# Expert tiles of a mixture of experts: 32 full tiles and four units of two half tiles in place of 39 tiles

## The reference, cut to what matters

```python
h = _L0_tok_ref(x, ...)                      # moving averages, then 128 -> 256
h = h + _L0_attn_ref(_layernorm(h), ...)
h = h + _L0_ffn_ref(_layernorm(h), ...)      # the experts
h = h + _L1_attn_ref(_layernorm(h), ...)
h = h + _L1_ffn_ref(_layernorm(h), ...)

def _L0_ffn_ref(x, gate_w, gate_b, w1, b1, w2, b2):
    probs = jax.nn.softmax(x_flat @ gate_w.T + gate_b, axis=-1)
    topk_vals, topk_idx = jax.lax.top_k(probs, 2)
    h = jax.nn.relu(jnp.einsum('nd,edh->neh', x_flat, w1) + b1)     # 256 -> 1024
    y = jnp.einsum('neh,eho->neo', h, w2) + b2                      # 1024 -> 256
    out_flat = jnp.einsum('ne,neo->no', dense_gate, y)
```

## Time and profile before

| what | before |
| --- | --- |
| median of 3 runs | 763.72 us |
| span of the profiled execution | 773.7 us |
| mean granted TensorE clock in it | 0.964 |
| TensorE busy | 701.8 us, 91% |
| VectorE, ScalarE, GpSimd busy | 444.4, 350.6, 147.4 us |
| expert stage, first to last product | 247.0 to 543.8 us |
| its 39 tiles | 7.24 us each in the steady part |
| attention, layer 1 | 543.8 to about 735 us |

### The profile page before, as it was taken

One profiled execution on the slowest core, in us unless ns is written; L12 is line 12 of the kernel. 1 busy time (PEld: TensorE's weight loads), 2 busy tenths in 40 slices (PEclk: granted clock), 3 DMA queues, 4 the chain that ended last, 5 costly groups with the idle time before them and its releaser, 6 DMA issues.

```text
span 773.7 us, 16147 instructions
## 1 busy us (share of the span) xinstructions
PE 701.8 (91%) x5671; PEld 576.0 (74%) x5681; DVE 444.4 (57%) x1129; ACT 350.6 (45%) x599; POOL 147.4 (19%) x180
## 2 busy tenths in 40 slices
PE   5697999999889999999999999999889999999855
PEld 4476777777767998999999999998556666665533
DVE  3567587778763542244322232233479988977686
ACT  2242453355335221212211212131779898899735
POOL 2010112331322021000000100200465553411000
PEclk9799999999998999999999999999999999999975
DMA  6979264466374566555555555574555774555002
GB/s 166 201 138 271 41 91 89 76 89 89 76 171 159 183 195 239 196 184 197 161 187 198 188 187 198 173 184 115 93 88 73 110 107 67 81 63 69 1 14 96
DMA packets 70839, 102.54 MB, mean 133 GB/s; under 512 B 8416, under 2 KB 58600, under 8 KB 70640
## 3 DMA queue, kind: packets, MB, share of 16 engines
q1 hardware_dynamic: 67376, 93.15, 50.4%
q0 software_dynamic: 3136, 8.40, 4.3%
q10 hardware_dynamic: 256, 0.07, 0.0%
HBM read 63.75 MB, written 12.58 MB: 99 GB/s over the span
## 4 chain that ended last, share of the span: by engine, by line
PE 65%; DVE 12%; DMA 8%; issue 5%; ACT 4%; POOL 2%; SPq 2%; ACTq 0%; DVEq 0%; POOLq 0%
PE psum L2102 18%; PE psum L2153 17%; DMA arena<-arena 7%; PE psum L2060 3%; PE psum L1782 3%; PE psum L2045 3%; PE psum L2074 3%; DVE arena L1346 2%; DVE arena L1199 2%; PE psum L1806 2%; POOL w0T L703 2%; PE psum L2051 1%; SPq L568 1%; PE psum L1811 1%; PE psum L2130 1%
## 5 line engine op out<-in xcount | busy, mean ns | idle before, releaser
L2102 PEld LDWEIGHTS psum<-arena 128*128 128x128 f32 x1248 | 144.9, 192 | 3.3 <-issue 1.7
L2102 PE MATMUL psum<-arena 128*128 128x128 f32 x1248 | 146.1, 275 | 1.2 <-issue 1.1
L2153 PE MATMUL psum<-arena 128*128 x624 | 141.3, 380 | 0.8 <-DVE arena L1492 0.8
L875 ACT ACTIVATE arena<-psum,arena 128x128 f32<-128x128 f32 x156 | 44.5, 368 | 190.1 <-PE psum L2102 106.6
L2153 PEld LDWEIGHTS psum<-arena 128*128 128x128 f32 x624 | 115.6, 190 | 15.3 <-issue 1.2
L1474 DVE TENSOR_SCALAR arena<-psum,arena 128x128 f32<-128x128 f32 x156 | 44.0, 344 | 81.0 <-PE psum L2102 64.8
L2060 PE MATMUL psum<-arena 96*128 96x256 bf16 x512 | 74.8, 276 | 8.4 <-ACT arena L845 4.2
L1346 DVE TENSOR_TENSOR arena<-arena 128x1024 f32<-128x1024 f32 x64 | 77.9, 1284 | 1.3 <-ACT arena L845 1.3
L1199 DVE TENSOR_REDUCE arena<-psum 128x6 f32<-128x768 f32 x64 | 59.3, 954 | 28.9 <-PE psum L1811 27.5
L703 POOL DMA_INDIRECT w0T<-yg,pos x32 | 40.3, 1260 | 185.6 <-DMA yg<-arena 177.4
L2060 PEld LDWEIGHTS psum<-arena 96*128 96x128 bf16 x512 | 44.8, 98 | 40.5 <-issue 14.7
(11 more groups left out here) (309 smaller groups left out, 1201.4 us busy)
## 6 DMA issues: line engine op xcount, KB each, us to landing
arena<-in_L_ffn_w_dram SPq DMA_DIRECT2D x47, 1024.0 KB
arena<-arena SPq DMA_DIRECT2D x192, 128.0 KB, 4.6
arena<-xg SPq DMA_DIRECT2D x39, 128.0 KB
yg<-arena SPq DMA_DIRECT2D x39, 128.0 KB, 1.7
out_dram<-arena SPq DMA_DIRECT2D x8, 256.0 KB, 2.1
xg<-zeros SPq DMA_DIRECT2D x9, 128.0 KB, 2.6
arena<-in_x_dram SPq DMA_DIRECT2D x8, 128.0 KB, 3.2
arena<-in_L_ffn_b_dram SPq DMA_DIRECT2D x1, 1024.0 KB
```

The lines of the kernel that those rows point to most:

```text
L875: ins = act.activation(hidT[:, v, c, :], psum[:, 2 * v, c * P:(c + 1) * P], ACT.Relu, bias=b1c[:, v, c:c + 1])
L2102: mm = pe.matmul(psum[:, 2 * v + c // HALF, (c % HALF) * P:(c % HALF + 1) * P], w1b[:, i % W1_BUFS, d, c * P:(c + 1) * P], xtT[:, v, d, :] ...
L2153: mm = pe.matmul(y_bank, hidT[:, u, c, :], w2s[:, one(e), c, :].rearrange("p o n -> p (o n)"), start=(c == 0), stop=(c == HC - 1))
```

## The change

**Units.** An expert's remainder of at most 64 rows goes to a half tile, one of over 64 to a full one. Then 32 full tiles and 8 half tiles suffice for any routing, and where more than 32 full ones would be needed, the surplus takes two halves each. Two half tiles, of two experts, make a pair. The stage runs 36 units: 8 early full tiles, then four times three full tiles and a pair (units 11, 15, 19 and 23), then 12 full tiles.

**A pair's first layer** has the tokens stationary (64 of them for each half) and the weights moving: 8 products of 512 columns, alternating between the halves, whose results stand in PSUM rows 0 to 63 and 64 to 127. ScalarE and VectorE copy these to `hid_raw`, TensorE transposes them back (8 transposes, behind the second layer of the unit before), and then each half gets the bias and relu of its own expert, 8 operations of 64 columns on each engine. The second layer is 16 products of 256 columns, alternating; the second half's weights are copied by VectorE to `w2p` before. A pair loads two sets of first-layer weights, with a fourth buffer `w1p` until the last pair has begun, and two blocks of 64 rows.

**The plan** sorts the late tiles so that those that the first three batches need come among the first 13, and lists 40 entries. `late_valid` has 7 steps where it had 3, `late_grid` 16 where it had 3, `late_list` 6 where it had 5; `slot_levels` has 8 steps where it had 4, `slot_counts` 8 where it had 6, `half_counts` is new with 3, and `tile_slots` has 17 where it had 7, now in iteration 15. `rank_tokens` keeps a copy of the counts for four batches of the first stage.

**Gathers.** The gather of batch 0 waits for 24 units, those of batches 1 and 2 for 25, and that of batch 3, for all 36, stands right behind that of batch 2, ahead of the attention's iterations. Combining and statistics of batch 2 are among the tiles now (iterations 33 and 34), and the steps of batches 0 and 1 are moved to fit. In the first stage the step that negated the row maxima is gone; the sign is applied in a copy on ScalarE.

```diff
+def unit_table():
+
+    units = [("full", t) for t in range(EARLY_TILES)]
+    for j in range(PAIR_UNITS):
+        units += [("full", EARLY_TILES + LEAD * j + n) for n in range(LEAD)] + [("pair", j)]
+    return units + [("full", t) for t in range(EARLY_TILES + LEAD * PAIR_UNITS, FULL_TILES)]
...
+    last, loads, table = [-1] * (W1_BUFS + 1), [0] * (W1_BUFS + 1), []
+    for i in range(UNITS):
+        mine = []
+        for _ in entries(i):
+            free = [n for n in range(W1_BUFS + (i < SPARE_UNTIL)) if last[n] != i]
+            n = min(free, key=lambda n: (last[n], n))
+            mine.append((n, loads[n] + 1, last[n] + 1))
+            last[n], loads[n] = i, loads[n] + 1
+        table.append(mine)
+    return table
...
-            e = sp.value_load(tile_e[0:1, i:i + 1], min_val=0, max_val=EXPERTS - 1)
-            sp.dma_start(w1b[:, i % W1_BUFS], a["L0_ffn_w1"][one(e), :, :].rearrange("o (c p) n -> p (o c) n", p=P)
-                         ).then_inc(w1_ld[i % W1_BUFS], 16)
+            for entry, (n, _, ready) in zip(entries(i), W1_OF[i]):
+                wait(sp, S["l1_hi"], ready)
+                e = sp.value_load(tile_e[0:1, entry:entry + 1], min_val=0, max_val=EXPERTS - 1)
+                sp.dma_start(w1_at(n), a["L0_ffn_w1"][one(e), :, :].rearrange("o (c p) n -> p (o c) n", p=P)
+                             ).then_inc(w1_ld[n], 16)
...
+            rows = P // len(entries(i))
+            for n, entry in enumerate(entries(i)):
+                r = sp.value_load(tile_row[0:1, entry:entry + 1], min_val=0, max_val=EXPERTS * CAP - P)
+                sp.dma_start(xt_in[n * rows:(n + 1) * rows, i % 2], xg[bass.ds(r, rows), :]).then_inc(x_ld[i % 2], 16)
...
-                    done = min(EARLY_TILES + 2 * EXPERTS, MOE_TILES) if b == 0 else min(2 * EXPERTS * (b + 1), MOE_TILES)
+                    late = FIRST_OF_0 if b == 0 else FIRST_TILES if b < FIRST_BATCHES else LATE_TILES
+                    done = LATE_ROW + late
...
-                for b in range(2):
+
+                for b in range(3):
                     gather(b)
                     scale1(b, 0, S["n_mv"], S["n_eps"], S["n_rstd"])
-                gather(2)
+                gather(3)
...
+                    pair = pair_of(i + 1)
+                    if pair is not None:
+                        act.wait_ge(S["l1_lo"], i + 2)
+                        wait(act, S["hid_mm"], pair)
+                        act.copy(hid_raw[:, 0:HID // 2], psum[:, 2 * v, :]).then_inc(S["hid_ev"], 1)
...
+                    if pair is not None:
+                        act.wait_ge(S["bias_done"], i + 2)
+                        act.wait_ge(S["hid_mm"], pair + 1)
+                        act.wait_ge(S["l2_mm"], i)
+                        for c in range(HALF):
+                            for n, bias in enumerate((b1c[:, v], b1p)):
+                                ins = act.activation(hidT[:, v, c, n * HALF_P:(n + 1) * HALF_P],
+                                                     psum[:, 2 * v, c * P + n * HALF_P:c * P + (n + 1) * HALF_P], ACT.Relu,
+                                                     bias=bias[:, c:c + 1])
+                        ins.then_inc(S["reluA"], 1)
...
+                    plan(dve.tensor_reduce(plan_s[:, 0:3], plan_place.rearrange("p (k e) -> p k e", e=EXPERTS), AX, ALU.add))
+                    plan(dve.tensor_reduce(plan_s[:, 3:6], plan_total.rearrange("p (k e) -> p k e", e=EXPERTS), AX, ALU.add))
+                    plan(dve.tensor_copy(plan_of[:], plan_total.rearrange("p (k e) -> p k e", e=EXPERTS)))
+                    plan(dve.tensor_tensor(plan_of[:, 0:2], plan_of[:, 0:2], over(chosen_of[:], 1, [P, 2, EXPERTS]), ALU.add))
+                    plan(dve.tensor_scalar(place_t, before_t, total_n, before_n, ALU.add, ALU.subtract))
...
+                    if pair is not None:
+                        a_e, b_e = (expert_of(entry) for entry in entries(i + 1))
+                        wait(dve, S["reluA"], i)
+                        dve.tensor_copy(b1c[:, v, :], b1T[:, :, one(a_e)].rearrange("p c o -> p (c o)"))
+                        dve.tensor_copy(b1p, b1T[:, :, one(b_e)].rearrange("p c o -> p (c o)")).then_inc(S["bias_done"], 1)
+                        dve.wait_ge(S["bias_done"], i + 2)
+                        dve.wait_ge(S["l1_hi"], i + 2)
+                        dve.tensor_copy(hid_raw[:, HID // 2:], psum[:, 2 * v + 1, :]).then_inc(S["hid_ev"], 1)
+                        wait(dve, S["l2_mm"], i)
+                        dve.tensor_copy(w2p, w2s[:, one(b_e)].rearrange("p o c n -> p (o c) n"))
...
+                        rows = P // len(entries(i))
+                        for n, entry in enumerate(entries(i)):
+                            e = expert_of(entry)
+                            at = slice(n * rows, (n + 1) * rows)
+                            ins = dve.tensor_tensor(yt[at, u], y_bank[at], b2r[at, one(e), :].rearrange("p o d -> p (o d)"), ALU.add)
+                        ins.then_inc(S["y_ev"], 1)
+                    if pair is not None:
+                        dve.wait_ge(S["hid_mm"], pair + 1)
+                        for c in range(HALF, HC):
+                            for n, bias in enumerate((b1c[:, v], b1p)):
+                                lo = (c - HALF) * P + n * HALF_P
+                                ins = dve.tensor_scalar(hidT[:, v, c, n * HALF_P:(n + 1) * HALF_P],
+                                                        psum[:, 2 * v + 1, lo:lo + HALF_P], bias[:, c:c + 1], 0.0, ALU.add, ALU.max)
+                        ins.then_inc(S["reluD"], 1)
...
                         tile_slots()
+                    if i == 25:
+                        combine(0)
+                        stat1(0)
                     if i == 26:
-                        combine(0)
-                    if i == 27:
-                        stat1(0)
+                        norm1(0)
                     if i == 28:
-                        norm1(0)
-                    if i == 32:
+                        combine(1)
+                        stat1(1)
...
+                    if i == 31:
+                        split_last(0, 1, S["n_km"], S["n_kl"])
+                        norm1(1)
+                    if i == 32:
+                        biased_v(0, 0)
+                    if i == 33:
+                        combine(2)
                     if i == 34:
-                        split_last(0, 1, S["n_km"], S["n_kl"])
...
+                        stat1(2)
...
-                    if b == 0:
-                        combine(2)
-                        stat1(2)
...
+                    if pair_of(i) is not None:
+                        for g in range(2):
+                            for d in range(DC):
+                                for n in range(2):
+                                    at = slice(n * HALF_P, (n + 1) * HALF_P)
+                                    mm = pe.matmul(psum[at, 2 * v + g, :], xtT[:, v, d, at],
+                                                   w1_at(W1_OF[i][n][0])[:, d, g * HID // 2:(g + 1) * HID // 2],
+                                                   start=(d == 0), stop=(d == DC - 1))
+                            if g == 0:
+                                mm.then_inc(S["l1_lo"], 1)
+                        mm.then_inc(S["l1_hi"], 1)
+                        return
...
+                        rows = P // len(entries(i))
                         for c in range(HC):
-                            mm = pe.matmul(y_bank, hidT[:, u, c, :],
+                            mm = pe.matmul(y_bank[0:rows], hidT[:, u, c, 0:rows],
                                            w2s[:, one(e), c, :].rearrange("p o n -> p (o n)"), start=(c == 0), stop=(c == HC - 1))
+                            if rows < P:
+                                mm = pe.matmul(y_bank[rows:P], hidT[:, u, c, rows:P], w2p[:, c, :],
+                                               start=(c == 0), stop=(c == HC - 1))
                         mm.then_inc(S["l2_mm"], 1)
+                    if pair_of(i + 1) is not None:
+                        pe.wait_ge(S["hid_ev"], 2 * (pair_of(i + 1) + 1))
+                        for c in range(HC):
+                            mm = pe.transpose(psum[:, 2 * (1 - u) + c // HALF, (c % HALF) * P:(c % HALF + 1) * P],
+                                              hid_raw[:, c * P:(c + 1) * P], ident[:])
+                        mm.then_inc(S["hid_mm"], 1)
```

323 lines of the change are left out of this document (199 added, 124 removed).

## The result

| | median us | runs | lowest to highest |
|---|---|---|---|
| before, same occasion | 763.80 | 4 | 763.48 to 765.53 |
| changed | 755.88 | 4 | 750.76 to 758.67 |
| ratio | 0.9857 | | 95% interval 0.9816 to 0.9897 |

The change gains 7.9 us. The first of these jobs had 756.37 (6 runs) against 764.92 (26 runs): 8.6 us less, ratio 0.9883 (0.985 to 0.9916). I had forecast 19.9 us, and 739.0 to 750.5 us: the time lies above the range, and less than half of the gain came.

A forecast was written before the change was run, and what follows sets the result against it. The prediction took TensorE, busy 91% of the span and without a gap in the expert stage, as the bound. Its terms, -21.7 + 4.2 + 1.0 + 0.7 - 4.1 = -19.9 us, gave 743.8 us, range 739.0 to 750.5.

The forecast's parts named there:

- three tiles fewer: Expert stage: 39 tiles become 36 units, each 7.24 us, all on the path; -21.7 us.
- four pairs: Expert stage: each pair takes 8.3 us, 1.05 more than a full tile; +4.2 us in all.
- late plan: After unit 4, VectorE's longer chain of steps delays TensorE's list of candidates; +1.0 us, bounds 0 and +3.
- placing, other waits of the stage: Expert stage: longer token-placing blocks exceed the slack in two places, 0.35 us each; +0.7 us, bounds 0 and +2.
- change-over and second attention: Attention behind the expert stage: earlier combining and gathering remove waits; -4.1 us, with no term for the change-over.
- first stage: Before the tiles: one VectorE step per batch goes, a small copy comes in four batches; 0, bounds -1 and +1 us.
- rival 1: Expert stage: a pair's halves run one after the other, 14.9 us a pair, 770.2 us in all; chance 5%.
- the remainder: A pair's layers: switching TensorE's tiling mode in and out costs 0.15 us for each layer beyond full overlap.
- Attention starts with more done: Second attention: batch 2 combined and batch 3 gathered earlier; -1.6 and -2.5 us in two batches, bounds 0 and -6.5.
- the sign of being wrong: Second attention batch: forecast near 23 us; staying at 25 would show the forecast wrong.
- rival 3: Attention: TensorE waits as long for ScalarE as it did for VectorE; 4.1 us less gain, 747.9 us; chance 12%.
- The anchor: Whole kernel: the profiled span of 773.7 us lies 10.0 above the 763.7 median; the difference was taken over unscaled.

The follow-up runs named there:

- a_cands: The changed kernel with the late list's product moved behind unit 6's first layer; 755.29 us.
- a_spread: The changed kernel with the 17 steps of the last placing block cut in two, 7 in iteration 15 and 10 in iteration 16; 755.06 us.
- a_late: The changed kernel with batch 2's combining and batch 3's gather put back in the attention's first iteration; 755.36 us against 756.37 with the part in.
- a_late32: The changed kernel with batch 2's combining and batch 3's gather put back and the arena on a multiple of 512 bytes; 743.30 us.
- b_pad96: The kernel before with 96 unused bytes ahead of the arena, which then starts 480 beyond a multiple of 512; 767.25 us, ratio to before 1.0014.
- a_pad416: The changed kernel with 416 unused bytes ahead of the arena, which then starts 384 beyond a multiple of 512, as in before; 754.41 us.
- a_best: The changed kernel with the arena on a multiple of 512, the last placing block in two and the late product behind unit 6's first layer; 740.20 us.
- a_pad32: The changed kernel with 32 unused bytes ahead of the arena, which then starts on a multiple of 512; 741.22 us, ratio to before 0.9708.

## Why the forecast was wrong, by its own steps

| step | forecast | shown | by |
|---|---|---|---|
| three tiles fewer | -21.7 | -21.7 | units of 7.24 us |
| four pairs | +4.2 | +5.6 | 1.39 each |
| late plan | +1.0 | +2.2 | unit 5; a_cands |
| placing, other waits of the stage | +0.7 | +1.7 | units 14, 17, 18; a_spread for unit 17 |
| change-over and second attention | -4.1 | -0.4 | +0.6 and -1.0 in the two traces; a_late, a_late32 |
| first stage | 0 | +3.5 | layout 1.0 to 2.8, the rest new code; b_pad96, a_pad416 |
| tail | 0 | +0.3 | two traces |
| sum | -19.9 | -8.8 | two traces; medians -7.9 and -8.6 |

**Right.** The bound of the expert stage, the period of 7.24 us, the full overlap of a pair's halves (rival 1 is dead: 3.59 and 3.61 us a layer), the pair's copies hidden under TensorE's work (no wait ahead of the transposes or behind them), and the weights' copy: 1.22 us, between my bounds of 1.1 and 1.7. By the Trainium skill ("VectorE: DVE Perf Modes", section Mode 2x_2P) I had estimated 1.1; the trace agrees nearly.

**Mis-sized: a pair.** By the remainder from the earlier trace rows I charged its two layers 0.03 and 0.15 us more than a full tile's; they cost 0.02 and 0.16. What I had not counted are 0.10 us on the layer ahead, 0.10 on the layer behind, and 0.14 on the transposes of coming tiles beside its layers. The Trainium skill ("TensorEngine Tiling (Array Packing)", section Key Properties) says that changing the mode drains the engine; the timeline agrees at both seams, 3.55 for 3.45 and 3.67 for 3.57 us, but no run separates a drain from other causes. The bounds of 8.0 to 9.5 held (7.24 + 1.39 = 8.63).

**Mis-sized: the late plan.** I let its steps overlap with the 1.11 us of the earlier trace rows, a wait which the trace I read had and the six other traces of before's code had not. Against the trace I read, +1.0 was right (8.73 to 9.70); against the others it is +2.2. The steps themselves were longer, too: 16 took 3.7 us where 3 took 0.6 (3.1 more, counted 2.6). The bound of +3 held.

**Mis-sized: the placing.** I counted 0.35 us where the 17 steps follow a pair; it was 1.17, since the bias copy, the relu and two evictions queue behind each other there. And `slot_levels`, of which I priced nothing, went from 4 steps to 8, and 0.41 us of idle time show behind it (unit 14).

**The steps that failed in kind.** There are two, and they are the largest parts of the miss.

The first is "Attention starts with more done", -4.1 us. The waits in the earlier trace rows did go, as the text said, but I took ScalarE as the only thing that would be late next. In the second batch, forecast at 23.1 us, a transfer within the arena was: TensorE waits 2.4 us for such transfers in a_cands, and the batch takes 24.8, the 25 that I had named as the sign of being wrong. Without them it takes 23.7 (a_best), and the two batches together give 2.8 of the 4.1. In the first batch TensorE waits longer for ScalarE, as my rival 3 said. The time came out near what that rival took from the gain, but in the second batch not by its mechanism. The change-over, which I had left out, took 0.6 us more: TensorE waits 1.45 us for VectorE's result where it waited 0.84, and no run tells why.

The second is "the first stage: 0, bounds -1 and +1". It counted instructions only. The new tiles' 608 bytes ahead of the arena were in the diff, and I did not ask what they move. That is 1.0 to 2.8 of the 3.5 us. The layout was poor before the change already. With the arena at 480 beyond a multiple of 512 in both codes the change is worth 10.9 us, at 0 in both 15.0. The attention's part explains 1.6 of these 4.1 us (1.8 against 0.2); with 4 runs of each kernel at 0 the rest is not settled. a_pad32, at 741.22 us, lies inside my range. That would have been luck: nothing in the sum stands for the 15 us that the layout gave it.

**The anchor.** That my profile stood 12 us above the other executions' spans did not spoil the sum, since I took a difference; what spoiled a term was a wait read from it. I wrote that "the engines' times are the same in both as far as I can tell"; the pace of the first stage was not, 186.3 us for seven batches where others have 177.3.

## What to carry to other kernels

A change that adds tiles ahead of a buffer that transfers use also moves that buffer: work out its start before and after, and put it on a multiple of 256 bytes. Before pricing a change on one trace, take a second one of the same kernel; a wait that carries a term should be in both. When small costs meet in one iteration (evictions, a block of steps, a bias, a relu on one engine), add them in queue order: a block cut in two cost nothing and gave 1.2 us in the stage's trace.

## Of the hardware

- The same 93.15 MB took the DMA engines 49.0, 51.5 or 53.3% of the span by where the arena starts (0, 384 or 480 bytes beyond a multiple of 512), and 48.6% at 256; the kernel before ran in 756.17, 765.18, 767.25 and 756.76 us.
- A layer of TensorE with two groups of 64 columns side by side runs in 3.59 (first layer) and 3.61 us (second) where the same layers with 128 take 3.57 and 3.45, and the layer ahead of the pair and the one behind it take 0.10 us more each.
- One kernel had an execution in which the same loop ran at another pace: seven batches in 186.3 us once, in 177.3 and 177.7 in two others of the same layout. From 99.5 to 206 us the granted clock was 1.00 in the slow one. Why is open.
